# Cross-attention kernel: the values of the first two pairs of key tiles in one visit, in the eleventh slot of a step

## The reference, cut to what matters

```
xs = layernorm(src)                       # src: 8 x 750 x 512
k2, v2 = split(xs @ ed_wkv)               # by heads
q2 = layernorm(tgt + self_attention) @ ed_wq
wei2 = softmax(q2 @ k2.T * scale)         # 224 x 750 for each head
ed_out = (wei2 @ v2) @ ed_wproj + ed_bproj
```

## The kernel before, in words

| kind | fills |
|---|---|
| 0 | V in 0, 1; K in 2 to 5; E in 6, 7 and in 9, 10 (from the third batch on) |
| 1 | K in 0 to 3; V in 4, 5, 8, 9 |
| 2 | K in 0 to 3; V in 5, 6, 8, 9; ACT normalises the next batch's context (`normalise`, L1613) in 4 to 7, 9, 10 |
| 3 | K in 0 to 3; V in 4, 5; T in 4 to 11 (of these steps, 7 have value items of pair 0 and 1 besides) |

## Time and profile before

### The profile page before, as it was taken

How to read it: one execution, slowest core, us unless ns; L and a number is a source line. 1 busy time by engine, 2 the same in 40 slices (tenths; PEclk the granted TensorE clock), 3 DMA queues, 4 the chain that set the end, 5 groups by cost and what they waited for, 6 DMA issues and landing times.

```text
span 1372.2 us, 24578 instructions
## 1 busy us (share of the span) xinstructions
PE 1310.9 (96%) x9193; PEld 1082.5 (79%) x9193; DVE 794.4 (58%) x2007; ACT 662.1 (48%) x1609; POOL 701.5 (51%) x577
## 2 busy tenths in 40 slices
PE   7999999999899999998788999999999999999997
PEld 6888888888788888887677787878877787887874
DVE  6613223232777777776655575756757566575565
ACT  5311111232666665666433656474665647456444
POOL 3232221322444555556733767666676766667661
PEclk9999999999999999999599999999999999999999
DMA  7400102114647776547267685777677587766641
GB/s 237 145 18 16 62 31 77 46 60 117 139 86 178 166 186 148 122 123 185 63 142 119 100 128 98 132 123 125 101 127 120 101 137 104 142 101 112 90 71 41
DMA packets 100400, 151.67 MB, mean 111 GB/s; under 512 B 10197, under 2 KB 63229, under 8 KB 99514
## 3 DMA queue, kind: packets, MB, share of 16 engines
q1 hardware_dynamic: 100282, 150.11, 53.8%
HBM read 66.74 MB, written 24.12 MB: 66 GB/s over the span
## 4 chain that ended last, share of the span: by engine, by line
PE 76%; POOL 8%; issue 5%; DVE 5%; DMA 3%; ACT 2%; SPq 1%; POOLq 0%; ACTq 0%; DVEq 0%
PE ps L1727 18%; PE ps L453 11%; PE ps L164 10%; PE ps L423 10%; PE ps_pair L1744 6%; PE ps L1759 5%; PE ps L1773 5%; PE ps L1832 3%; POOL ca_partial L1586 2%; DMA ca_k_stack<-ca_keys 2%; POOL ca_xT L1473 1%; DMA sa_K_stack<-sa_rows 1%; PE ps L1207 1%; PE ps L1791 1%; PE ps L1227 1%
## 5 line engine op out<-in xcount | busy, mean ns | idle before, releaser
L1664 DVE TENSOR_REDUCE ca_maxes<-ps 112x1 f32<-112x375 f32 x512 | 256.5, 541 | 106.0 <-PE ps L1759 103.9
L1607 ACT ACTIVATE ca_probT<-ps_pair 125x448 f32<-125x448 f32 x384 | 210.3, 554 | 181.5 <-PE ps_pair L1744 179.6
L1586 POOL TENSOR_TENSOR ca_partial<-ca_partial,ca_probT 125x896 f32<-125x896 f32 x118 | 249.2, 2112 | 93.6 <-ACT ca_probT L1607 89.0
L312 POOL TENSOR_TENSOR ff_hT<-ff_hrelu,ff_hT 128x512 fp32r<-128x512 f32 (+1 forms) x64 | 77.9, 1218 | 203.2 <-DVE ff_hT L394 203.2
L1759 PE MATMUL ps<-ca_k_stack,ca_q_stack 96*112 96x376 f32 x512 | 168.7, 352 | 6.9 <-issue 3.6
L1744 PEld LDWEIGHTS ps_pair<-ca_q_stack,ca_k_stack 98*125 98x125 f32 x768 | 130.2, 186 | 44.0 <-issue 31.9
L1744 PE MATMUL ps_pair<-ca_q_stack,ca_k_stack 98*125 98x224 f32 x768 | 156.2, 285 | 1.3 <-ACT ca_probT L1607 1.2
L423 PE MATMUL ps<-ff_w,ff_hT 128*128 128x512 f32 x672 | 155.5, 390 | 0.0
L1727 PE MATMUL ps<-w_b,ca_xT 128*125 128x512 f32 x576 | 151.2, 398 | 3.1 <-POOL ca_xT L1473 2.5
L1727 PE MATMUL ps<-ca_xT,w_a 128*128 128x376 f32 x768 | 153.1, 335 | 0.0
L423 PEld LDWEIGHTS ps<-ff_w,ff_hT 128*128 128x128 f32 x672 | 125.6, 188 | 25.8
(11 more groups left out here) (145 smaller groups left out, 2433.0 us busy)
## 6 DMA issues: line engine op xcount, KB each, us to landing
ca_k_stack<-ca_keys SPq DMA_DIRECT2D x96, 376.0 KB, 8.0
sa_Q_stack<-sa_rows SPq DMA_DIRECT2D x96, 112.0 KB, 3.5
sa_K_stack<-sa_rows SPq DMA_DIRECT2D x96, 112.0 KB, 3.7
ca_q_stack<-q_out SPq DMA_DIRECT2D x96, 112.0 KB, 9.5
ctx_tokens<-in_ctx_dram SPq DMA_DIRECT2D x14, 672.0 KB
ctx_tokens<-in_L_xattn_ff_w_dram SPq DMA_DIRECT2D x16, 512.0 KB, 4.4
q_out<-sa_yT SPq DMA_DIRECT2D x16, 448.0 KB, 3.7
wp_lo<-wp_out SPq DMA_DIRECT2D x6, 1024.0 KB, 4.8
```

The lines of the kernel that those rows point to most:

```text
L312: pool.tensor_tensor(hT[:, LO, m % RING, 0:width(g)], hrelu[i % 2][:, 0:width(g)], hT[:, HI, m % RING, 0:width(g)].bitcast(F32), ALU.subtr ...
L1586: pool.tensor_tensor(total, total, half(a), ALU.add).then_inc(partial_done, 1)
L1607: act.activation(probT[u // GH][0:JT, u % GH].rearrange("p a t -> p (a t)"), ps_p[u % 2][0:JT, 0:2 * T], ACT.Exp).then_inc(exp_done, 1)
L1664: dve.tensor_reduce(maxes[:, q, j, a:a + 1], ps_s[n % 3][0:TQ, 0:JH], AX_X, ALU.max).then_inc(s_read, 1)
```

## The change

The value items of pair 0 and pair 1 were put at the end of slot 7 and of slot 10. Both now stand at the end of slot 10, pair 0 first. No other item moves, and no wait or instruction is added or taken out.

```diff
 NORMALISE = (4, 5, 6, 7, 9, 10)
 LAST_D = 4
+FIRST_VALUES = 10
 LAST_E = {0: ((5, 2, 1, 0), (6, 2, 1, 1), (8, 2, 1, 2), (9, 2, 1, 3)),
@@ in plan_cross_attention @@
             if i == 3 and keys:
                 items.append(("queries", s))
-            if i in (7, 10) and 0 <= s - 3 < NG:
-                items.append(("value", s - 3, (i - 7) // 3))
+            if i == FIRST_VALUES and 0 <= s - 3 < NG:
+                items += [("value", s - 3, pair) for pair in range(2)]
             if now and b + 1 < B:
                 if b > 0 and (g, i) in STATISTICS:
```

## The result

The changed kernel takes 1373.52 us (median of 20 runs, 1370.87 to 1377.31) against 1370.96 us (20 runs, 1369.25 to 1373.74): ratio 1.0018, 95% interval 1.0012 to 1.0024, or +1.6 to +3.3 us. The interval leaves out 1, so the changed kernel is slower, but by 0.18%, just under the 0.2% that the prediction took for what can be told from no change.

What follows compares the result with a forecast made beforehand. TensorE, busy 96% of the span, sets the time by its order of work. Terms -1.9 + 0.7 + 1.4 + 1.9 + 0.3 + 0.05 + 1.2 = +3.7 us on 1370.09 give 1373.8; 8-in-10 range 1369.0 to 1376.5.

Steps and rivals of the forecast that it cites:

- way in and out: TensorE's switch into and out of a value item's tile shape; saving one gains 0.31 us a step if nothing waits.
- The cost of a visit taken out: Slot 7: removing one value item's 16 matmul records saves TensorE 1.09 us between scores.
- the second behind the first: Slot 10: the second value item's 16 records directly behind the first add 0.78 us, bounded by 0.61 and 0.89.
- Kind 1 and step 30: Steps with s % 4 = 1, and one without normalising: 1.02 us saved, -0.24 each, 8 steps, -1.9 us.
- Kind 2 with normalising: Six steps: slot 8's prob item waits for ACT's exponential, only 0.66 us saved; +0.12 each, +0.7 us.
- Kind 0: Six s % 4 = 0 steps with output projection: slot 9's score waits for DVE's read behind the residual; +0.23 each, +1.4 us.
- Kind 3: Seven steps with transposes: ACT is full, nothing saved, and the double visit delays V; +0.27 each, +1.9 us.
- Steps 4 and 31: Two steps paced by DVE's score reads throughout: 0.65 us saved, +0.13 each, +0.3 us together.
- The last two: Steps 33 and 34, without scores: the double visit delays slot 11's prob item; +0.7 and about +0.5, +1.2 us.
- Rival A: Faster: waits in slots 8 and 9 don't bind, as queues hold more than counted; 1364.2 us, chance 0.13.
- B: No change: V's delay from the double visit goes and the last two steps' cost is halved; 1371.3 us, chance 0.22.
- C: Slower still: the second value item's semaphore waits break the run, costing 0.89 instead of 0.78; 1377.3 us, chance 0.09.

Runs made afterwards that it cites:

- e7: The changed kernel measured once more, not altered; 1372.74 us, ratio 1.0013 against the kernel before.
- e2: The changed kernel with slot 10's second score put between the two value items; 1381.07 us, ratio 1.0070 against before.
- e4: The changed kernel with DVE's residual addition put behind the slot's second score instead of ahead of it; 1371.32 us, ratio 0.9994 against before.
- e6: The changed kernel with ACT's normalising moved from slots 4, 5, 6, 7, 9, 10 to 4, 8, 8, 9, 9, 10; 1371.93 us, ratio 1.0000 against before.
- e9: The changed kernel with only steps 33 and 34 put back to value items in slots 7 and 10; 1372.14 us, ratio 1.0000 against before.

## Why the prediction was right, point by point

The forecast, +3.7 us and slower, held in sign; in size it was too high. The runs say +2.6 (+1.6 to +3.3), the steps +1.7 in e7 (+1.8 with step 3) and +3.3 in the one profile with the slow clock. That 1373.8 was forecast and 1373.52 measured is closer than the reasoning deserves: the forecast stood on a median of 3 runs, 1370.09, and the median of 20 is 0.9 us higher. The mechanism, a saved way in and out against uncovered waits, is shown by e2 for the gain, by e4 and e6 for two of the waits, and by e9 for the weight of the last two steps. The delay in kind 3 is read from the trace; no run isolates it. Term by term:

- The cost of a visit taken out (1.09) and of the second behind the first (0.78): 0.76 measured, and e2 gives 0.29 to 0.36 for the way in and out.
- Kind 1 and step 30, -1.9: measured 7 steps at -0.27 and -0.17, -2.0. Two slips cancel here, which is luck. The prediction took the second record of the pair in the earlier trace rows for 0.33 us long; it had waited and lasts 0.43, so s2(7) starts at 956.52, 0.05 after the read that releases it, not 0.14. By 0.05 s1(8) would have been free at 956.98 and saved 1.09 in all, the whole visit; the 0.07 that is missing sits in the late weight load.
- Kind 2 with normalising, +0.12 each: +0.12. The cause, an exponential behind normalising in ACT's queue, is shown by e6.
- Kind 0, +0.23 each: +0.14. The place was right (e4). The price was too high: the release from DVE's read to the score takes 0.05 us (935.80 to 935.85), not the 0.14 that was misread from the pair in kind 1; and 0.02 is the 0.76.
- Kind 3, +0.27 each: +0.14. V came later as forecast, 0.24 us by the shift of V less the shift of the transposes at ACT's pace (922.97 to 920.33, and 919.73 to 916.85). But the wait that V no longer has also gave back 0.06: after it, the weights were not loaded ahead, and V to p1 took 1.47 us where it now takes 1.41. Another 0.03 went at D, 0.81 us behind the visit before and 0.78 after, where the loader had waited 0.27 us for POOL's sum and now waits 0.15. The prediction said that nothing would come back there.
- Steps 4 and 31, +0.13 each: -0.05 and +0.02. DVE's reads follow one another at 0.454 us where nothing interrupts them, not 0.46 to 0.475, and the release is 0.05 here too. Ten reads in a row, in step 4 of the changed kernel:

```profile
773.26 4.63 DVE L1665 TENSOR_REDUCE ca_maxes<-ps 112x1 f32<-112x375 f32 x10
```

- The last two, +1.2: +1.3 in all profiles with the pair in slot 10 and a full clock. By e9 they make up nearly the whole net cost. This shifts the weight of the explanation: the forecast had 2.5 us in the steady steps and 1.2 at the end, and the measured steps have 0.5 and 1.3. The 1.9 us between are in three terms: kind 0, kind 3 (0.9, the largest), and steps 4 and 31.

Rival A (faster) falls with the waits at s1(9), p8 and the transposes. B (no delay in kind 3) was half right in size, not in mechanism. C falls: the second visit begins 0.76 us after the first. What the prediction said would be seen, six new waits for DVE's read, six for ACT's exponential in kind 2 and none for POOL at V, is there; that steps of kinds 0 and 3 would be some 0.25 us longer is not, they are 0.14 longer.

## What to carry to other kernels

Putting two visits to a rare tile shape together saves one way in and out, here 0.33 us, but each visit was also the time in which other engines caught up. Before moving one, read for every kind of step what waits stand behind the place that it leaves, with the depth of the banks; a place that pays in one kind (slot 8 in kind 0) can cost 1 us in another. Look at the last steps apart: there nothing covers the long visit.

## What was not expected of the hardware

- The granted clock fell to 0.50 for some 3 us in one of five profiles of the same last steps, after the same wait of 0.7 us, and cost 1.6 us (step 33: +2.29 against +0.65). What sets it off is not shown.
- A wait of PE costs more than its length: the weights behind it are not loaded ahead, so p to the next score takes 0.31 us instead of 0.22, and a V fill to p1 1.47 instead of 1.41 (its first weights came at 922.94, 0.03 ahead of the matmul).
